# A fused attention and ternary feed-forward kernel: TensorE's units of a round in another order

## Chip, cores and metric

One core of a Trainium2 chip runs the whole kernel. The metric is device time of one execution in microseconds (us), the median of several runs. The profile is of one further execution with its own time.

## What is computed

The input x has 4 batches of 1024 rows of 128 numbers. The rows are normalised (xn) and go through causal attention with 16 heads of width 64 and through a linear layer with a ternary matrix and quantised input; both results are added to x.

```python
xn = _layernorm(x)
# attention
q, k, v = heads(xn @ Wq), heads(xn @ Wk), heads(xn @ Wv)
w = softmax(q @ k.T / DH + causal)
w = w * mask                       # a ramp over the keys, one span per head
w = w / (sum(w) + 1e-08)
att = (w @ v) @ Wo
# feed-forward
x_int = clip(round(xn / scale), -127, 127)
ffn = nan_to_num(x_int * scale) @ (ternary_weight - 1).T + bias
out = x + att + ffn
```

## The kernel before, in words

**Pairs and rounds.** Two heads of one batch make a pair: 4 batches of 8 pairs, 32 pairs in all. The plans at the top of the file (lines 36 to 54) give each engine's order for one round of the loop; a `+` or `-` behind a name means the next or the last pair. While the scores of pair i are worked on, the projections and maxima of pair i+1 are made and the division and output of pair i-1 are finished. `walk` (line 90) expands the plans; the FIRST plans run ahead of round 0, the LAST plans replace the plans in the last round. Nothing is scheduled at run time: each engine takes its units in the written order, and semaphores hold a unit back.

**The units on TensorE (PE).** Q and K are projections of a pair (lines 937 to 941, six matmuls each with 512 columns), V the values (lines 955 to 957, twelve of 256). M0 to M11 are products for the row maxima (line 968, one matmul for each of the two heads, side by side in the array). S0 to S11 are the score tiles (line 1006, four such pairs of matmuls; the exponent's shift is subtracted as the fourth). G3, G7 and G11 multiply four probability tiles each with the values (line 1023), D0 and D1 sum the denominators of each half of the queries (line 1038), Y0 and Y1 multiply the normalised values with Wo (line 1065; for the last pair of a batch the feed-forward's products at line 1053 go first). T turns the maxima (lines 975, 976), X0 and X1 turn the normalised rows of the next batch, four 128-column transposes each (line 922), W turns the ternary matrix once (line 1110).

**Shapes of the array.** Q, K, V, T, X, W and Y use the array as 128 x 128 (shown as 128\*128, T as 128\*16). M and S use it as two arrays of 64 rows (64\*128), one for each head. G and D use two arrays of 64 columns (128\*64). In program order TensorE changes between these three kinds fourteen times a round.

**The ring.** Q, K, V, M and S write to three slots of PSUM, two banks each, in turn (`IN_RING`, `NSLOT` = 3). A unit may start only when the unit three places before it in the ring has been read out: a score tile by ScalarE's exponential (E, line 567, with `exp_done`), a maximum by VectorE (R, lines 768 and 772, with `max_read`), V by VectorE's weighted copy (Vs, line 755, `v_done`), Q and K by VectorE's remainder (line 744). A further bank, `beside`, holds T, D, Y, X and W in turn, and `pv` holds the products of G. In `slot_left` (line 881) and `beside_left` (line 898) stand these waits.

```python
unit, j = IN_RING[n - NSLOT]
if unit[0] == "S":
    pe.wait_ge(exp_done, tiles_upto(j, int(unit[1:])))
elif unit[0] == "M":
    pe.wait_ge(max_read, j * NM + int(unit[1:]) + 1)
```

**The other engines.** ScalarE (ACT) makes the high parts of Q and K (line 556), the exponentials, and logarithm and inverse of the denominators (ln, ex, lines 573 and 578). VectorE (DVE) makes the remainders, the maxima R0 to R11 (R0 to R3 and R8 to R11 by two custom instructions with a mask, R4 to R7 by one reduction of 1024 numbers), the weighted values Vs, two steps of division (t, u, lines 792 and 797), the normalised values (o, line 804), the sum into the output (Ya, line 813) and one of seven steps of the quantisation for each pair (q, lines 700 to 712). GpSimd (POOL) zeroes the upper triangle of diagonal tiles (L, line 474), sums the probabilities over keys (A, lines 497 and 501) and adds the bias (B, line 463).

**Rows of the next batch.** In rounds 4 and 5 of a batch, X0 and X1 are turned into `beside`; ScalarE copies each half twice (high part, whole value `xf`), and VectorE makes the remainder.

Of the kernel before, what the change touches and what calls it, by code (L numbers as in the profile page):

```python
# [5 lines left out]
ALU = mybir.AluOpType  # L6
# [26 lines left out]

PE_PLAN = ("T Q+ K+ X0 X1 W G11- M0+ M1+ S0 S1 S2 M2+ D1- M3+ S3 V+ S4 S5 M4+ S6 M5+ Y1- M6+ M7+ S7 D0 G3 "
           "M8+ S8 S9 S10 M9+ Y0 M10+ M11+ S11 G7")
ACT_PLAN = "Z Qhi+ Khi+ X0 X1 E0 E1 E2 ln1- ex1- E3 E4 E5 E6 E7 ln0 ex0 E8 E9 E10 E11"
DVE_PLAN = ("Tc Z Qlo+ Klo+ R0+ R1+ X0 X1 W R2+ R3+ t1- u1- Vs+ o1- R4+ R5+ Ya1- R6+ R7+ t0 u0 R8+ o0 q "
            "R9+ R10+ Ya0 R11+")  # L40
POOL_PLAN = "L0 A0 L1 A1 L2 A2 L3 A3 A4 A5 A6 A7 L8 L9 L10 L11 A8 A9 A10 A11 B"

PE_FIRST = ("Q+ K+ I0+ I1+ M0+ M1+ M2+ I2+ M3+ I3+ M4+ I4+ M5+ I5+ H+ M6+ I6+ M7+ I7+ M8+ I8+ M9+ I9+ M10+ I10+ "
            "M11+ S0+ S1+ T+ S2+ S3+ Q++ K++ V+")
DVE_FIRST = ("Qlo+ Klo+ R0+ R1+ R2+ R3+ R4+ Hc+ R5+ R6+ R7+ R8+ R9+ R10+ R11+ Tc+ keys+ scale+ "
             "Qlo++ Klo++ Vs+")
ACT_FIRST = "xf0+ Qhi+ xf1+ Khi+ keys+ rest+ Hrow+ wv+ E0+ E1+ E2+ E3+ Qhi++ Khi++"


PE_LAST = "T G11- S0 S1 S2 D1- S3 S4 S5 S6 Y1- S7 D0 G3 S8 S9 S10 S11 Y0 D1 F1 G7 G11 Y1"  # L50
POOL_LAST = "L0 A0 L1 A1 L2 A2 L3 A3 L8 L9 L10 L11"
DVE_LAST = "Tc t1- u1- o1- A5 Ya1- A6 A7 t0 u0 o0 A8 A9 Ya0 t1 u1 o1 Ya1"
SP_PLAN = "mrow kext+ store-"
SP_FIRST = "kext+"

# [10 lines left out]
           8: "rstd2", 9: "norm2a", 10: "norm2b", 11: "norm3a", 12: "norm3b"}  # L66


def happens(name, i):

    if name in ("X0", "X1"):
        return i % PAIRS_OF_BATCH == 4 + int(name[1:]) and i < N_PAIRS - PAIRS_OF_BATCH
    if name == "W":
        return i == 1
    if name == "F1":
        return i == LAST
    if name[0] == "I":
        return i == 0
    if name == "q":
        return i % PAIRS_OF_BATCH < PAIRS_OF_BATCH - 1  # L80
    if name == "Z":
        return i in STEP_OF
    if name == "B":
        return i in (6, 11, 14)
    if name == "store":
        return i % PAIRS_OF_BATCH == PAIRS_OF_BATCH - 1
    return True
# [15 lines left out]


PE_ORDER = list(walk(PE_PLAN, PE_FIRST, PE_LAST))
IN_RING = [("X", -2)] + [u for u in PE_ORDER if u[0][0] in "QKSMV" or u == ("D1", LAST)]
IN_BESIDE = [u for u in PE_ORDER if u[0][0] in "THDYXWF" and u not in (("D1", LAST), ("Y1", LAST))]
PLACE = {u: n for n, u in enumerate(IN_RING)}
PLACE_BESIDE = {u: n for n, u in enumerate(IN_BESIDE)}
NSLOT = 3  # L110
# [20 lines left out]
def attention_ffn(nc, x_dram, wq_dram, wk_dram, wv_dram, wo_dram, span_dram, tern_dram, bias_dram,  # L131
# [11 lines left out]
    with ctx:  # L143
# [243 lines left out]
        def _(pool):  # L387
# [75 lines left out]
                g.tensor_tensor(rows, rows, bias_b[:, :].unsqueeze(1).to_broadcast([P, KB, P]), ALU.add  # L463
                                ).then_inc(bias_added, 1)

            pool.wait_ge(maxrow_done, 1)
            add_bias(0)

            def select(i, t):

# [33 lines left out]
            for name, i in walk(POOL_PLAN, "", POOL_LAST):  # L504
                if name[0] == "L":
                    select(i, int(name[1:]))
                elif name[0] == "A":
                    add(i, int(name[1:]))
                else:
                    add_bias((6, 11, 14).index(i) + 1)  # L510

        @block.scalar
        def _(act):
# [29 lines left out]
            def turned_whole(b, c, src):

                if b > 0:
                    act.wait_ge(fq_step, (b - 1) * FQ_STEPS + 1)
                else:
                    act.wait_ge(x2_done, c + 1)
# [47 lines left out]
            for name, i in walk(ACT_PLAN, ACT_FIRST):  # L596
                if name in ("Qhi", "Khi"):
                    high_parts(i, i % 2, name[0])
                elif name[0] == "E":
                    exps(i, int(name[1:]))  # L600
                elif name[:2] == "ln":
                    logarithms(i, int(name[2:]))
                elif name[:2] == "ex":
                    inverses(i, int(name[2:]))
                elif name[0] == "X":
                    turned_high(batch_of_turn(i), int(name[1:]), beside[:, :])
                    turned_whole(batch_of_turn(i), int(name[1:]), beside[:, :])
                elif name[:2] == "xf":
                    turned_whole(0, int(name[2:]), ring[:, slot("X", -2), int(name[2:]), :])
                elif name == "rest":  # L610
                    for n in range(2):
                        weights(w1[n][:, P:H * DH], w_raw[n][:, P:H * DH], w_rest_landed, 32, w_hi_done)
                elif name == "keys":
                    key_logarithms()
                elif name == "Hrow":
                    act.wait_ge(ext_done, 16 * NEXT)
                    act.wait_ge(first_rows_done, 1)
                    for h in range(2):
                        act.dma_start(mrow[0][h * DH:h * DH + 1, 0:HALF].bitcast(F32),
                                      first_rows[:, h * P:(h + 1) * P].bitcast(F32)).then_inc(first_rows_landed, 16)  # L620
                elif name == "wv":
                    weights(wv1[:, :], wv_raw, wv_landed, 16, wv_hi_done)
                elif STEP_OF[i] == "var1+":
                    rstd_start(2, slice(KB, 2 * KB))
                elif STEP_OF[i] == "rstd2":
                    rstd_start(3, slice(2 * KB, NB))

        @block.vector
        def _(dve):
# [40 lines left out]
            def turned(b, c, src):  # L670

                cols = slice(c * HALF, (c + 1) * HALF)
                dve.wait_ge(x1_done if b == 0 else xf_done, 2 * b + c + 1)
                v.tensor_tensor(x2[b % 2][:, cols], src, x1[b % 2][:, cols].bitcast(F32), ALU.subtract
                                ).then_inc(x2_done, 1)

# [165 lines left out]
            for name, i in walk(DVE_PLAN, DVE_FIRST, DVE_LAST):  # L842
                if name in ("Qlo", "Klo"):
                    low_parts(i, i % 2, name[0])
                elif name == "Vs":
                    weighted_values(i)
                elif name[0] == "R":
                    maxima(i, i % 2, int(name[1:]))
                elif name == "Tc":
                    maxima_out(i)  # L850
                elif name == "Hc":
                    first_rows_out()
                elif name == "scale":
                    quantisation_scale()
                elif name[0] == "A":
                    add_last(int(name[1:]))
                elif name[0] == "t":
                    newton_first(i, int(name[1:]))
                elif name[0] == "u":
                    newton_second(i, int(name[1:]))  # L860
                elif name[0] == "o":
                    normalise_values(i, int(name[1:]))
                elif name[:2] == "Ya":
                    add_output(i, int(name[2:]))
                elif name == "q":
                    quantise(i // NPB, i % NPB + 1)
                elif name[0] == "X":
                    turned(batch_of_turn(i), int(name[1:]), beside[:, :])
                elif name == "Z":
                    layer_norm_rest(STEP_OF[i])  # L870
                elif name == "keys":
                    key_weights()
                else:
                    dve.wait_ge(ternT_ready, 1)
                    v.tensor_copy(ternT[:, :], beside[:, 0:P]).then_inc(ternT_done, 1)

        @block.tensor
        def _(pe):
            t_ = nc.tensor

            def slot_left(name, i):
# [9 lines left out]
                elif unit in "QK":  # L891
                    pe.wait_ge(low_done, 2 * j + "QK".index(unit) + 1)
                elif unit == "V":
                    pe.wait_ge(v_done, j + 1)
                else:
                    pe.wait_ge(xf_done, 2)

            def beside_left(name, i):

# [9 lines left out]
                    pe.wait_ge(rden_done, halves_upto(j, int(unit[1:])))  # L909
                elif unit[0] == "Y":  # L910
                    pe.wait_ge(y_added, halves_upto(j, int(unit[1:])))
                elif unit[0] == "X":
                    pe.wait_ge(x2_done, 2 * batch_of_turn(j) + int(unit[1:]) + 1)
                else:
                    pe.wait_ge(ternT_done, 1)

# [161 lines left out]
            for name, i in PE_ORDER:  # L1078
# [57 lines left out]
```

## Time and profile before

| | |
|---|---|
| median of 3 runs | 1001.96 us (1001.88 to 1002.1) |
| profiled execution, its own time | 1001.64 us |
| its span in the profile | 999.9 us |
| TensorE busy | 985.0 us (99%) |
| VectorE busy | 757.3 us (76%) |
| GpSimd busy | 707.5 us (71%) |
| ScalarE busy | 451.7 us (45%) |
| mean granted TensorE clock | 0.997 |

Matmuls overlap in the records: one of 512 columns is shown as about 0.39 us long, and the next pair starts 0.23 us after it. So a busy TensorE says only that something is in the array; what a unit costs is read from start to start. Two matmuls of one unit that lie side by side in the array start within 0.01 us of each other. The timeline merges consecutive instructions of one form into one row with their count.

### The profile page before, as it was taken

Reading aid. Unit: us, or ns where it says so; the run is one execution under the profiler, and the core shown is the slowest. Engines: PE = TensorE matmul, PEld = TensorE weight load, DVE = VectorE, ACT = ScalarE, POOL = GpSimd, SP = SyncE. Lnnn points to the kernel's source line nnn. Section 1 sums busy time; section 2 is a strip of 40 time slices with the busy share of each in tenths; the row PEclk is TensorE's granted clock in tenths of the full one; section 3 lists DMA queues with packets and bytes.
Section 4 is the critical chain, followed back from the end, with each engine's and each line's share of the span. In section 5 each row is a group of like instructions: output and inputs, shape, how many; then the busy total and the mean of one; then the engine's idle time right before and its main releaser. Section 6 shows DMA issues by size and latency. Waiting matters only on the chain.

```text
span 999.9 us, 19209 instructions
## 1 busy us (share of the span) xinstructions
PE 985.0 (99%) x7121; PEld 634.2 (63%) x7121; DVE 757.3 (76%) x1706; ACT 451.7 (45%) x607; POOL 707.5 (71%) x649
## 2 busy tenths in 40 slices
PE   8899999999999999999999999999999999999997
PEld 4666666666666666666666666666666666666654
DVE  7877888878788878777767777777877667777754
ACT  4344445444454444454443454444454444454442
POOL 8766867667767668767767767667767667777672
PEclk9999999999999999999999999999999999999999
DMA  6000000000000000000000000000000000000000
GB/s 176 3 2 2 2 1 3 2 3 2 2 22 3 2 2 2 1 3 2 3 12 13 1 3 2 2 2 3 1 2 23 3 2 2 1 2 2 2 2 22
DMA packets 16133, 8.52 MB, mean 9 GB/s; under 512 B 5404, under 2 KB 15644, under 8 KB 16040
## 3 DMA queue, kind: packets, MB, share of 16 engines
q1 hardware_dynamic: 15416, 7.15, 2.7%
q8 instruction: 57, 0.93, 0.4%
q14 instruction: 36, 0.29, 0.1%
q10 hardware_dynamic: 624, 0.14, 0.1%
HBM read 4.33 MB, written 2.10 MB: 6 GB/s over the span
## 4 chain that ended last, share of the span: by engine, by line
PE 87%; DVE 8%; issue 2%; POOL 1%; ACT 1%; DMA 1%; DVEq 0%; SPq 0%; ACTq 0%; POOLq 0%
PE pv L1023 25%; PE ring L1006 24%; PE ring L968 12%; PE beside L1065 7%; PE beside L1038 6%; PE ring L941 3%; PE ring L937 3%; PE ring L938 3%; DVE ring L768 3%; DVE v L755 2%; DVE beside L792 1%; PE ring L955 1%; PE beside L1053 1%; PE ring L956 1%; PE ring L957 1%
## 5 line engine op out<-in xcount | busy, mean ns | idle before, releaser
L567 ACT ACTIVATE prob<-ring 128x1024 f32<-128x1024 f32 (+3 forms) x384 | 293.6, 810 | 347.9 <-PE ring L1006 347.7
L501 POOL TENSOR_TENSOR psumd<-psumd,prob 128x512 f32<-128x512 f32 (+1 forms) x250 | 406.4, 1626 | 28.9 <-POOL psumd L501 1.3
L768 DVE CUSTOM_DVE_ANT_0 ring<-ring,causal 128x128 f32<-128x128 f32 (+3 forms) x512 | 240.3, 517 | 96.7 <-PE ring L968 96.2
L1006 PE MATMUL ring<-q,k 64*128 64x512 f32 (+3 forms) x2304 | 279.5, 347 | 1.7 <-DMA mrow<-maxrow 0.8
L1023 PE MATMUL pv<-prob,v 128*64 128x512 f32 (+3 forms) x1536 | 267.1, 490 | 0.0
L474 POOL TENSOR_SCALAR_AFFINE_SELECT prob<-prob 128x256 f32<-128x256 f32 x256 | 110.1, 432 | 216.1 <-ACT prob L567 214.1
L1006 PEld LDWEIGHTS ring<-q,k 64*128 64x128 f32 x2304 | 194.6, 185 | 37.3 <-DVE rowmax L768 5.1
L1023 PEld LDWEIGHTS pv<-prob,v 128*64 128x64 f32 x1536 | 104.9, 137 | 154.1 <-issue 142.4
L772 DVE TENSOR_REDUCE rowmax<-ring 128x2 f32<-128x1024 f32 x128 | 151.5, 1222 | 4.8 <-PE ring L968 1.3
L497 POOL TENSOR_TENSOR psumd<-prob 128x768 f32<-128x768 f32 (+1 forms) x63 | 132.6, 2105 | 24.3 <-ACT prob L567 19.1
L968 PE MATMUL ring<-k,q 64*128 64x512 f32 (+3 forms) x768 | 143.9, 410 | 4.2 <-DVE k L744 1.5
L1006 PE MATMUL ring<-mrow,kext 64*128 64x512 f32 (+3 forms) x768 | 133.6, 342 | 0.0
L968 PEld LDWEIGHTS ring<-k,q 64*128 64x128 f32 x768 | 64.9, 184 | 74.2 <-ACT prob L567 27.7
L556 ACT ACTIVATE q<-ring 128x1024 fp32r<-128x1024 f32 x32 | 32.9, 1028 | 143.6 <-PE ring L941 143.6
L1006 PEld LDWEIGHTS ring<-mrow,kext 64*128 64x128 f32 x768 | 73.2, 185 | 7.7
L1065 PE MATMUL beside<-wo,o 128*128 128x128 f32 x512 | 73.4, 286 | 1.1 <-DVE o L804 1.1
L768 DVE DVE_READ_ACCUMULATOR2_ANT rowmax<- 128x1 f32 x512 | 72.5, 142 | 0.0
L1065 PEld LDWEIGHTS beside<-wo,o 128*128 128x128 f32 x512 | 62.0, 191 | 13.9 <-issue 9.2
L792 DVE TENSOR_TENSOR beside<-beside,r 128x512 f32<-128x512 f32 x63 | 45.0, 715 | 32.9 <-ACT r L578 32.8
L744 DVE TENSOR_TENSOR q<-ring,q 128x1024 fp32r<-128x1024 f32 x32 | 39.1, 1222 | 40.1 <-ACT q L556 40.0
L1038 PE MATMUL beside<-psumd,ones 128*64 128x512 f32 x252 | 68.0, 617 | 0.9 <-POOL psumd L501 0.9
L937 PE MATMUL ring<-x,w 128*128 128x512 f32 x128 | 53.0, 414 | 0.0
(120 smaller groups left out, 947.0 us busy)
## 6 DMA issues: line engine op xcount, KB each, us to landing
kext<-kext SPq DMA_DIRECT2D x128, 4.0 KB, 1.7
out<-x_sb SPq DMA_DIRECT2D x8, 256.0 KB, 2.4
x_sb<-in_L_attn_query SPq DMA_DIRECT2D x3, 512.0 KB, 5.5
mrow<-maxrow SPq DMA_DIRECT2D x62, 4.0 KB
x_sb<-in_L_attn_query SPq DMA_DIRECT2D x2, 256.0 KB, 4.0
xn_sb<-in_L_attn_Wv SPq DMA_DIRECT2D x1, 512.0 KB, 5.5
wo<-in_L_attn_Wo SPq DMA_DIRECT2D x1, 512.0 KB, 7.0
xn_sb<-in_L_attn_Wq SPq DMA_DIRECT2D x1, 448.0 KB, 3.5
```

The source lines that it names most:

```text
L474: g.affine_select(out=d, in_=d, compare_op=ALU.is_ge, fill=0.0, base=0, pattern=[[0, 2], [1, P]], channel_multiplier=-1).then_inc(sel_done, 1)
L497: g.tensor_tensor(acc[:, :, lo:HALF], before[:, :, lo:HALF], pr[:, :, lo:HALF], ALU.add).then_inc(acc_done, 2)
L501: g.tensor_tensor(acc[:, :, lo:HALF], acc[:, :, lo:HALF], pr[:, :, lo:HALF], ALU.add).then_inc(acc_done, 1)
L567: a.activation(prob[n % NPROB][:, :, lo:HALF], ring[:, slot(f"S{t}", i), :, lo:HALF], ACT.Exp, scale=1.0 / DH).then_inc(exp_done, 1)
L768: last = v.tensor_tensor_reduce(out=ring[:, s, h, 0:n], in0=ring[:, s, h, 0:n], in1=causal[:, HALF - n:HALF], scale=1.0, scalar=MASKED, op ...
L772: last = v.tensor_reduce(dst[:, :, 0], ring[:, s, :, 0:n], axis=AX, op=ALU.max)
L937: t_.matmul(ring[:, s, c, :], w1[n][:, cols], xa[:, rows], start=True, stop=False)
L968: last = t_.matmul(ring[:, s, h, 0:n], q1[p][rows, j * P:(j + 1) * P], k1[p][rows, k0:k0 + n], start=True, stop=True)
L1006: last = t_.matmul(ring[:, s, h, lo:HALF], k[p][rows, keys], q[p][rows, cols], start=(at == 0), stop=(at == len(parts) - 1))
L1023: last = t_.matmul(pv[h * DH:(h + 1) * DH, lo:HALF], v_sb[i // 2 % 2][:, kb, i % 2 * 2 + h, :], prob[(i * NT + t) % NPROB][:, h, lo:HALF], ...
L1038: last = t_.matmul(out[h * DH:(h + 1) * DH, :], ones[:, :], psumd[c][:, h, :], start=True, stop=not direct)
L1065: last = t_.matmul(beside[:, k * P:(k + 1) * P], o_sb[c][:, k * P:(k + 1) * P], wo[:, i % NPB, :], start=not with_ffn, stop=(not with_ffn ...
```

## The change

All of it is order, except for the turned rows. In a round, D1 of the last pair follows G11 at once; S3 and S4 follow S2; M2 and M3 come behind S4; Y1 and V follow M3 (with X, if there is one); S7 comes ahead of M6 and M7. The changes of the array's shape in a round are then: into G11 and D1, into M0, into Y1 and V, into S5, into D0, into M8, into Y0, into M10, into G7, into T, which is ten. VectorE's, ScalarE's and GpSimd's orders follow: q stands behind the remainder of K, R0 and R1 before t1, u1 and o1, R2 and R3 before Ya1 and Vs; ln and ex of the last pair stand before E0; A8 stands before L9.

X is now one unit of eight transposes in the ring, in round 4 of a batch. ScalarE makes only the high part from it; the whole value `xf` is made by GpSimd as the sum of both parts. In the first plans, S4 of pair 0 and M0 and M1 of pair 1 with two idle products between them are moved ahead of round 0, and the first bias comes behind A3 of pair 0.

```diff
-PE_PLAN = ("T Q+ K+ X0 X1 W G11- M0+ M1+ S0 S1 S2 M2+ D1- M3+ S3 V+ S4 S5 M4+ S6 M5+ Y1- M6+ M7+ S7 D0 G3 "
+PE_PLAN = ("T Q+ K+ G11- D1- M0+ M1+ S0 S1 S2 S3 S4 M2+ M3+ Y1- V+ X S5 M4+ S6 M5+ W S7 M6+ M7+ D0 G3 "
            "M8+ S8 S9 S10 M9+ Y0 M10+ M11+ S11 G7")
-ACT_PLAN = "Z Qhi+ Khi+ X0 X1 E0 E1 E2 ln1- ex1- E3 E4 E5 E6 E7 ln0 ex0 E8 E9 E10 E11"
-DVE_PLAN = ("Tc Z Qlo+ Klo+ R0+ R1+ X0 X1 W R2+ R3+ t1- u1- Vs+ o1- R4+ R5+ Ya1- R6+ R7+ t0 u0 R8+ o0 q "
-            "R9+ R10+ Ya0 R11+")
-POOL_PLAN = "L0 A0 L1 A1 L2 A2 L3 A3 A4 A5 A6 A7 L8 L9 L10 L11 A8 A9 A10 A11 B"
+ACT_PLAN = "Z Qhi+ Khi+ ln1- ex1- E0 E1 E2 E3 E4 X E5 E6 E7 ln0 ex0 E8 E9 E10 E11"
+DVE_PLAN = ("Tc Z Qlo+ Klo+ q R0+ R1+ t1- u1- o1- R2+ R3+ Ya1- Vs+ X R4+ W R5+ R6+ R7+ t0 u0 R8+ o0 R9+ "
+            "R10+ Ya0 R11+")
+POOL_PLAN = "L0 L1 L2 A0 L3 A1 A2 A3 B0 A4 A5 A6 A7 L8 A8 L9 L10 L11 A9 A10 A11 B xf"
@@
-            "M11+ S0+ S1+ T+ S2+ S3+ Q++ K++ V+")
+            "M11+ S0+ S1+ T+ S2+ S3+ Q++ K++ V+ S4+ M0++ I11+ M1++ I12+")
@@
-ACT_FIRST = "xf0+ Qhi+ xf1+ Khi+ keys+ rest+ Hrow+ wv+ E0+ E1+ E2+ E3+ Qhi++ Khi++"
-PE_LAST = "T G11- S0 S1 S2 D1- S3 S4 S5 S6 Y1- S7 D0 G3 S8 S9 S10 S11 Y0 D1 F1 G7 G11 Y1"
+ACT_FIRST = "xf0+ Qhi+ xf1+ Khi+ keys+ rest+ Hrow+ wv+ E0+ E1+ E2+ E3+ Qhi++ Khi++ E4+"
+PE_LAST = "T G11- D1- S0 S1 S2 S3 S4 Y1- S5 S6 S7 D0 G3 S8 S9 S10 S11 Y0 D1 F1 G7 G11 Y1"
@@
-DVE_LAST = "Tc t1- u1- o1- A5 Ya1- A6 A7 t0 u0 o0 A8 A9 Ya0 t1 u1 o1 Ya1"
+DVE_LAST = "Tc t1- u1- o1- q Ya1- A5 A6 A7 t0 u0 o0 A8 A9 Ya0 t1 u1 o1 Ya1"
@@
-IN_RING = [("X", -2)] + [u for u in PE_ORDER if u[0][0] in "QKSMV" or u == ("D1", LAST)]
-IN_BESIDE = [u for u in PE_ORDER if u[0][0] in "THDYXWF" and u not in (("D1", LAST), ("Y1", LAST))]
+IN_RING = [("X", -2)] + [u for u in PE_ORDER if u[0][0] in "QKSMVX" or u == ("D1", LAST)]
+IN_BESIDE = [u for u in PE_ORDER if u[0][0] in "THDYWF" and u not in (("D1", LAST), ("Y1", LAST))]
@@ gpsimd
-            pool.wait_ge(maxrow_done, 1)
-            add_bias(0)
+            def rows_of_parts(b):
+
+                pool.wait_ge(x2_done, 2 * b + 2)
+                pool.wait_ge(fq_step, (b - 1) * FQ_STEPS + 1)
+                g.tensor_tensor(xf[:, :], x1[b % 2][:, :].bitcast(F32), x2[b % 2][:, :].bitcast(F32), ALU.add
+                                ).then_inc(xf_done, 2)
@@ scalar
-                    turned_high(batch_of_turn(i), int(name[1:]), beside[:, :])
-                    turned_whole(batch_of_turn(i), int(name[1:]), beside[:, :])
+                elif name == "X":
+                    for c in range(2):
+                        turned_high(batch_of_turn(i), c, ring[:, slot("X", i), c, :])
@@ vector
-                dve.wait_ge(x1_done if b == 0 else xf_done, 2 * b + c + 1)
+                dve.wait_ge(x1_done, 2 * b + c + 1)
@@
-                    quantise(i // NPB, i % NPB + 1)
+                    quantise(i // NPB, i % NPB)
@@ tensor
+                else:
+                    pe.wait_ge(x2_done, 2 * batch_of_turn(j) + 2)
```

## Rows read from the trace of the kernel before

**Rows 1.** The page's first part: busy time, its share and instructions of each engine

```profile
PE 985.0 (99%) x7121; PEld 634.2 (63%) x7121; DVE 757.3 (76%) x1706; ACT 451.7 (45%) x607; POOL 707.5 (71%) x649
```

**Rows 2.** Timeline of PE, round of pair 18: start us, us, instruction, count

```profile
577.01 2.37 PE L1023 MATMUL pv<-prob,v 128*64 128x512 f32 x16
579.31 0.50 PE L968 MATMUL ring<-k,q 64*128 64x128 f32 x4
579.65 0.86 PE L1006 MATMUL ring<-q,k 64*128 64x512 f32 x6
...
581.85 0.44 PE L968 MATMUL ring<-k,q 64*128 64x384 f32 x2
582.23 1.08 PE L1038 MATMUL beside<-psumd,ones 128*64 128x512 f32 x4
583.24 0.50 PE L968 MATMUL ring<-k,q 64*128 64x512 f32 x2
583.57 0.45 PE L1006 MATMUL ring<-q,k 64*128 64x128 f32 x6
...
584.06 0.38 PE L955 MATMUL ring<-wv,x 128*128 128x256 f32 x1
...
585.68 0.98 PE L1006 MATMUL ring<-q,k 64*128 64x512 f32 x6
...
586.72 0.87 PE L1006 MATMUL ring<-q,k 64*128 64x512 f32 x6
...
587.84 0.51 PE L968 MATMUL ring<-k,q 64*128 64x512 f32 x2
588.19 0.85 PE L1006 MATMUL ring<-q,k 64*128 64x512 f32 x6
...
589.11 0.40 PE L968 MATMUL ring<-k,q 64*128 64x512 f32 x2
589.43 1.16 PE L1065 MATMUL beside<-wo,o 128*128 128x128 f32 x8
590.52 0.73 PE L968 MATMUL ring<-k,q 64*128 64x512 f32 x4
591.10 0.86 PE L1006 MATMUL ring<-q,k 64*128 64x512 f32 x6
...
592.11 0.65 PE L1038 MATMUL beside<-psumd,ones 128*64 128x512 f32 x2
```

**Rows 3.** Timeline of DVE in the same round

```profile
582.49 0.57 DVE L768 CUSTOM_DVE_ANT_0 ring<-ring,causal 128x384 f32<-128x384 f32 x1 [1.28 <-PE ring L968]
...
583.49 0.14 DVE L768 DVE_READ_ACCUMULATOR2_ANT rowmax<- 128x1 f32 x1
583.93 0.70 DVE L768 CUSTOM_DVE_ANT_0 ring<-ring,causal 128x512 f32<-128x512 f32 x1 [0.30 <-PE ring L968]
...
585.20 0.73 DVE L792 TENSOR_TENSOR beside<-beside,r 128x512 f32<-128x512 f32 x1
...
586.57 1.22 DVE L755 TENSOR_TENSOR v<-ring,vtab 128x1024 f32<-128x1024 f32 x1
...
588.50 2.39 DVE L772 TENSOR_REDUCE rowmax<-ring 128x2 f32<-128x1024 f32 x2
590.80 0.68 DVE L813 TENSOR_TENSOR x_sb<-x_sb,beside 128x512 f32<-128x512 f32 x1
```

**Rows 4.** Timeline of ACT: the first two exponentials of the same round, merged

```profile
580.77 1.73 ACT L567 ACTIVATE prob<-ring 128x1024 f32<-128x1024 f32 x2 [2.63 <-PE ring L1006]
```

**Rows 5.** Timeline of PE: the four transposes of an X unit, and G11

```profile
426.01 0.60 PE L922 MATMUL beside<-ident,xn_sb 128*128 128x128 f32 x4
426.54 2.37 PE L1023 MATMUL pv<-prob,v 128*64 128x512 f32 x16
```

**Rows 6.** Windows of round 0: length, busy us of each engine, clock, DMA share, GB/s

```profile
36.00:40.00 4.00, 2.41 (x13) 1.23 (x11) 4.00 (x12) 0.13 (x1) 3.83 (x5) 0.84 0.01 3
40.00:42.60 2.60, 2.60 (x14) 2.41 (x12) 2.34 (x9) 0.00 (x0) 0.62 (x1) 0.58 0.00 0
```

More of the change, by code:

```diff
@@ L66 @@
            8: "rstd2", 9: "norm2a", 10: "norm2b", 11: "norm3a", 12: "norm3b"}
+BIAS_AT = (0, 6, 11, 14)
 def happens(name, i):
-    if name in ("X0", "X1"):
-        return i % PAIRS_OF_BATCH == 4 + int(name[1:]) and i < N_PAIRS - PAIRS_OF_BATCH
+    if name in ("X", "xf"):
+        return i % PAIRS_OF_BATCH == (4 if name == "X" else 5) and i < N_PAIRS - PAIRS_OF_BATCH
     if name == "W":
@@ L79, in happens @@
     if name == "q":
-        return i % PAIRS_OF_BATCH < PAIRS_OF_BATCH - 1
+        return i % PAIRS_OF_BATCH > 0
     if name == "Z":
@@ L83, in happens @@
     if name == "B":
-        return i in (6, 11, 14)
+        return i in BIAS_AT[1:]
+    if name == "B0":
+        return i == BIAS_AT[0]
     if name == "store":
@@ L508, in _ @@
                     add(i, int(name[1:]))
+                elif name == "xf":
+                    rows_of_parts(batch_of_turn(i - 1))
                 else:
-                    add_bias((6, 11, 14).index(i) + 1)
+                    add_bias(BIAS_AT.index(i))
         @block.scalar
@@ L541, in turned_high, with turned_whole @@
                 a.activation(x1[b % 2][:, c * HALF:(c + 1) * HALF], src, ACT.Copy).then_inc(x1_done, 1)
[L543 to L548, printed above, removed]
+            def turned_whole(c, src):
+                act.wait_ge(x2_done, c + 1)
                 a.activation(xf[:, c * HALF:(c + 1) * HALF], src, ACT.Copy).then_inc(xf_done, 1)
@@ L604, in _ @@
                     inverses(i, int(name[2:]))
-                elif name[0] == "X":
-                    turned_high(batch_of_turn(i), int(name[1:]), beside[:, :])
-                    turned_whole(batch_of_turn(i), int(name[1:]), beside[:, :])
+                elif name == "X":
+                    for c in range(2):
+                        turned_high(batch_of_turn(i), c, ring[:, slot("X", i), c, :])
                 elif name[:2] == "xf":
-                    turned_whole(0, int(name[2:]), ring[:, slot("X", -2), int(name[2:]), :])
+                    turned_whole(int(name[2:]), ring[:, slot("X", -2), int(name[2:]), :])
                 elif name == "rest":
@@ L865, in _ @@
                 elif name == "q":
-                    quantise(i // NPB, i % NPB + 1)
-                elif name[0] == "X":
-                    turned(batch_of_turn(i), int(name[1:]), beside[:, :])
+                    quantise(i // NPB, i % NPB)
+                elif name == "X":
+                    for c in range(2):
+                        turned(batch_of_turn(i), c, ring[:, slot("X", i), c, :])
                 elif name == "Z":
@@ L894, in slot_left @@
                     pe.wait_ge(v_done, j + 1)
+                elif j < 0:
+                    pe.wait_ge(xf_done, 2)
                 else:
-                    pe.wait_ge(xf_done, 2)
+                    pe.wait_ge(x2_done, 2 * batch_of_turn(j) + 2)
             def beside_left(name, i):
@@ L911, in beside_left @@
                     pe.wait_ge(y_added, halves_upto(j, int(unit[1:])))
-                elif unit[0] == "X":
-                    pe.wait_ge(x2_done, 2 * batch_of_turn(j) + int(unit[1:]) + 1)
                 else:
@@ L1105, in _ @@
                     output_projection(i, int(name[1:]))
-                elif name[0] == "X":
-                    turn(batch_of_turn(i), int(name[1:]), beside[:, :])
+                elif name == "X":
+                    for c in range(2):
+                        turn(batch_of_turn(i), c, ring[:, slot("X", i), c, :])
                 else:
```

## The prediction, made before the changed kernel was run

> **What bounds the kernel now.** I read the page first: TensorE is busy 99% of the span, no other engine over 76% [rows 1]. That alone says little, because matmuls overlap in the records. So I took PE's timeline of one quiet round (pair 18, no turned rows, no feed-forward) and read every unit from start to start [rows 2]. It holds almost nothing but matmul work, and two kinds of small loss that the waits view hardly shows.
>
> The first loss is a change of the array's shape. M5's pair of 512 columns (589.11) is followed by Y1 after 0.32 us; four such pairs of S6 with its successor take 588.19 to 589.11, or 0.23 each. So the boundary costs 0.09. Behind it, the first step of the new shape is slow too: S4, first behind V, takes 1.04 (585.68 to 586.72), S6, in the middle of its stretch, 0.92. I call this 0.12 the refill. After D1, M3 takes 0.33 to S3 instead of 0.23. One change thus costs 0.2; into D and G the refill is smaller (I take 0.05), and out of them the boundary is 0.10.
>
> The second loss is a late slot. M4 starts at 587.84; VectorE's weighted values ended at 586.57 + 1.22 = 587.79 [rows 3]. S5 to M4 takes 1.12 instead of 0.92, so 0.20 is wait, and M4 to S6 takes 0.35 instead of 0.23: **a wait pays the refill again**. A unit starts 0.05 after the recorded end of its releaser.
>
> **What the new order gives.** It drops one entry into D1 (0.09 + 0.05), one exit from it (0.10 + 0.12) and one way into and out of 128 x 128 (2 x 0.21): 0.78 a round. M4's wait on V with its refill (0.32) also goes, since M4 now follows M3 in its slot. Together 1.10.
>
> The Trainium skill ("TensorEngine Tiling (Array Packing)", Key Properties) says that changing the tiling mode drains the engine; "TensorE: Matmul & The Clock Gate", Step-by-step, gives the array's drain as some 128 cycles. Estimated from these two pages a change would be 0.05 us at 2.4 GHz and four fewer would save 0.2 a round, 6 us in all, not 0.78 a round; the trace has durations for the boundary and for the refill, so they are used.
>
> **What it costs: three late slots.** A ring of three slots asks that a unit, and the two behind it, last as long as its read-out. I lay the new order out from G11 to D0, each term from one round [rows 2 to 4]:
>
> - G11 to D1: 2.30 less the boundary 0.10 = 2.20. D1 to M0: D1 to M3 is 1.01, less the refill 0.05 = 0.96. M0 to S0: 0.34.
> - S0 to S4: S4 takes the slot of S1 and needs E1. E1 ended at 580.77 + 1.73 = 582.50, 2.85 behind S0 [rows 2, 4], so S4 starts at 2.90. TensorE alone would be there at 2.64: S0 to S2 2.20 (579.65 to 581.85), S3 four pairs of 0.11. A wait of 0.26 appears. E0's release of S3 is as tight as it was for M2, which stood there.
> - S4 to M2: 1.04, refill included.
> - M2 to S6: S6 takes V's slot. VectorE starts R2 0.54 behind M2 (0.64 less the refill that M2 had), R2 takes 1.00 (582.49 to 583.49), R3 1.27 (583.93 to 585.20), Ya1 0.59 (0.68 less the 0.09 by which R5's end at 590.89 overlaps it), Vs 1.22; with 0.05 that is 4.67 [rows 3]. TensorE would need 4.29: M2 0.18, M3 0.32, Y1 1.00 (1.09 less its exit), V 1.52 (1.62 less its refill), S5 1.04, M4 0.23. Wait: 0.38.
> - S6 to M5: 0.92 + 0.12 = 1.04.
> - M5 to M7: M7 takes M5's slot and needs R5. M4 to R4 is 588.50 - 587.84 = 0.66, less 0.12 = 0.54; the reduction takes 1.24; with 0.05, 1.83. S7 and M6 between them fill only 0.23 + 0.92 + 0.23 = 1.38. Wait: 0.45. Before, Y1 lay here and gave the time.
> - M7 to D0: 0.32 and 0.11 of refill = 0.43.
>
> The sum is 15.41; the trace has 592.11 - 577.01 = 15.10. **A round gets 0.31 longer**: 1.10 gained, 0.26 + 0.38 + 0.45 waited and three refills (0.36) paid; without these 1.45 it would be 13.98, 1.12 shorter (the last 0.02 is rounding). Thirty rounds hold all of these units: +9.3.
>
> The same skill page (TensorEngine Tiling, Performance Considerations) warns that PSUM copies may become the bottleneck once TensorE is made faster by tiling. That speaks against this change in kind: every new wait above is a read-out. By the page alone there is no size.
>
> **The rest.** Everything behind D0 keeps its order on TensorE and nothing there is tight: 0. GpSimd's reordered tail only brings A11, and with it D1, forward: 0; were that cover gone, D1 would hold TensorE by what A11 lacks. The step q now lies between the remainder of K and R0; its longest form fits into the 0.86 (2.20 + 0.96 - 2.30) by which M0 comes later: 0, up to 0.1 in two rounds of eight. The first plan: S4's 1.04 goes into the stretch where TensorE is busy 2.41 of 4.00 us, and V, which ran behind it at a granted clock of 0.58, most of it at the lower level of 1.2 GHz, can run at the full 2.4 GHz; 2.60 x 0.42 = 1.09 is the most that this gives back [rows 6]. I take -2.1, bounds -2.3 and -0.5. The idle products lie in waits. Turned rows: two rounds of a batch each spent 0.53 - 0.09 = 0.44 on X [rows 5]; one round now spends 0.88, and the slot stays taken until ScalarE's and VectorE's two halves are through, which no row shows in this place. Bounds: -0.3 (X bridges V's wait) and +1.5 (two high parts and two remainders in series, less S5, M4); I take +0.3, three times: +0.9. GpSimd's sum for `xf` and the bias behind A3 move work on an engine with idle time: 0. Last round: two fewer changes, against score tiles that now follow each other and wait for exponentials; 0, bounds -0.6 and +1.
>
> Sum: 9.3 - 2.1 + 0.9 = +8.1 on the profiled 1001.64, that is 1009.7. The median of the runs lies 0.32 above the profiled time, so I forecast **1010 us**.
>
> **Rivals.**
> *Faster, the read-outs keep up.* Waits and refills of 1.45 decide against a gain of 1.12; with the -1.2 of the rest spread over the rounds the turning point is 1.16. If a slot were free well before the recorded end of its read-out, none of the waits would stand: 30 x -1.12 - 1.2 gives 967; with half of them left, 989. For it: engines other than TensorE idle a quarter of the time [rows 1]. Against it: M4 started 0.05 behind Vs to the hundredth, and M5 to M7 is a chain of three rows with no slack to find.
> *No change, the refill is not paid after these waits.* If the weights of S4, S6 and M7 are in before the release, 0.36 a round goes: 1010 - 10.8 = 999. M4 speaks against it.
> *Slower than forecast, turned rows.* At +1.5 a batch and with the start giving only 0.5, the sum is 1015.
> *The change does not do what it says.* Counting the plans gives ten changes; I give this nothing.
>
> **How the numbers follow.** Forecast case 0.58; refill not paid 0.13 (between 997 and 1003); more than forecast 0.09; read-outs keep up 0.20. Within 0.2% (2 us, about what a measurement of this kernel can tell from no change) is 1000 to 1004: 0.13. Slower: 0.66. Faster: 0.21. The forecast's own range is 1004 to 1014, from 0.1 a round in the terms and the bounds of the rest. To leave out no more than 2 in 10 it is stretched to 997 and 1015.
>
> **What would show it.** Right: D1 straight behind G11, and D0 15.4 behind G11; S4 0.05 behind the end of E1, S6 behind Vs, M7 behind R5, each followed by a slow first step; waits of score units on exponentials and of maxima on reductions; V of round 0 at the full clock. Wrong: S6 and M7 starting without a gap (first rival), or the gaps there with a first step of 0.23 (second).

## The result and the profile after

The changed kernel takes 1012.6 us (median of 4 runs, 1011.45 to 1018.1) where the kernel before takes 1001.92: a ratio of 1.0115, 95% interval 1.0091 to 1.0139. It is slower. The profiled execution has 1012.66 us and a span of 1010.9, 11.0 more than before.

The page first: busy times, then the chain that ended last by engine. TensorE is as busy as before [rows 1].

```profile
PE 987.0 (98%) x7125; PEld 627.2 (62%) x7125; DVE 751.9 (74%) x1706; ACT 452.2 (45%) x601; POOL 708.2 (70%) x652
...
PE 81%; DVE 11%; issue 4%; POOL 2%; ACT 1%; DMA 0%; SPq 0%; DVEq 0%; POOLq 0%; ACTq 0%
```

The last line, which read 87% for PE and 8% for DVE before, says where it goes: the chain runs more often through another engine. PE's timeline of the round of pair 18 shows the places, in the columns of [rows 2]:

```profile
579.23 2.37 PE L1032 MATMUL pv<-prob,v 128*64 128x512 f32 x16
581.43 1.03 PE L1047 MATMUL beside<-psumd,ones 128*64 128x512 f32 x4
582.39 0.50 PE L977 MATMUL ring<-k,q 64*128 64x128 f32 x4
...
585.63 0.96 PE L1015 MATMUL ring<-q,k 64*128 64x512 f32 x6
586.67 0.56 PE L977 MATMUL ring<-k,q 64*128 64x384 f32 x4
...
590.71 0.40 PE L977 MATMUL ring<-k,q 64*128 64x512 f32 x2
591.36 0.96 PE L1015 MATMUL ring<-q,k 64*128 64x512 f32 x6 [0.25 <-DVE v L763]
...
593.67 1.04 PE L977 MATMUL ring<-k,q 64*128 64x512 f32 x4
594.63 0.65 PE L1047 MATMUL beside<-psumd,ones 128*64 128x512 f32 x2
```

From the top: G11, D1, M0 and M1, ..., S4, M2 and M3, ..., M4, S6, ..., M6 and M7, D0. G11 to D0 takes 594.63 - 579.23 = 15.40 us; before it was 15.10. D1 stands directly behind G11. S4 waits for E1, ScalarE's second exponential:

```profile
584.78 0.80 ACT L575 ACTIVATE prob<-ring 128x768 f32<-128x768 f32 x1
```

It ends at 585.58, and S4 starts at 585.63. M4 (590.71) to S6 (591.36) is 0.65 instead of 0.23: S6 waits for the weighted values. M6 and M7 together last 1.04 in the merged row; M6 and M7 in [rows 2] lasted 0.73. VectorE's timeline shows who is late:

```profile
590.09 1.22 DVE L763 TENSOR_TENSOR v<-ring,vtab 128x1024 f32<-128x1024 f32 x1
591.26 1.23 DVE L780 TENSOR_REDUCE rowmax<-ring 128x2 f32<-128x1024 f32 x1
592.93 1.23 DVE L780 TENSOR_REDUCE rowmax<-ring 128x2 f32<-128x1024 f32 x1 [0.44 <-PE ring L977]
```

Vs ends at 591.31, S6 starts at 591.36. R5 ends at 594.16, and M7 can start only behind that; its row is merged, but 593.67 + 1.04 - 0.50 puts it at 594.21. VectorE itself idled 0.44 ahead of R5: TensorE and VectorE wait for each other in turn through three slots.

By stretches (start of T to start of T): the round of pair 0 went from 29.83 to 27.94 us (-1.89), the thirty rounds behind it from 902.96 to 911.22 (+8.26), the last round with the store from 36.40 to 41.04 (+4.64). Sum: 11.0.

The last round is a surprise. GpSimd's timeline of L1 and, further down, A3 in the kernel before:

```profile
970.69 0.41 POOL L474 TENSOR_SCALAR_AFFINE_SELECT prob<-prob 128x256 f32<-128x256 f32 x1
...
976.25 0.72 POOL L501 TENSOR_TENSOR psumd<-psumd,prob 128x256 f32<-128x256 f32 x1
```

And in the changed kernel:

```profile
977.06 1.29 POOL L483 TENSOR_SCALAR_AFFINE_SELECT prob<-prob 128x256 f32<-128x256 f32 x1
...
983.49 1.57 POOL L510 TENSOR_TENSOR psumd<-psumd,prob 128x256 f32<-128x256 f32 x1
```

The same select L1 takes 1.29 instead of 0.41, and the last sum A3 1.57 instead of 0.72. What VectorE does beside them, q's first step and then the sums A6 and A7:

```profile
976.77 1.36 DVE L720 COPY_PREDICATED fq<-xn_sb,big 128x1024 f32<-128x1024 uint32 x1
...
983.25 2.90 DVE L847 TENSOR_TENSOR psumd<-psumd,prob 128x1024 f32<-128x1024 f32 x2
```

D0 waits for A3. PE's timeline there, D0 and G3, before:

```profile
977.12 1.08 PE L1038 MATMUL beside<-psumd,ones 128*64 128x512 f32 x4 [0.85 <-POOL psumd L501]
978.00 2.35 PE L1023 MATMUL pv<-prob,v 128*64 128x512 f32 x16
```

The same after:

```profile
985.21 1.97 PE L1047 MATMUL beside<-psumd,ones 128*64 128x512 f32 x4 [3.62 <-POOL psumd L510]
986.95 4.40 PE L1032 MATMUL pv<-prob,v 128*64 128x512 f32 x16
```

And the windows of the wait and of D0 and G3 after (columns as in [rows 6]):

```profile
981.20:985.20 4.00, 0.40 (x4) 0.02 (x1) 3.79 (x3) 1.47 (x2) 3.79 (x3) 0.89 0.00 0
985.20:991.20 6.00, 5.99 (x20) 2.41 (x20) 2.34 (x3) 1.23 (x2) 0.00 (x0) 0.51 0.00 0
```

TensorE idled 3.62 us, and then ran D0 and G3 at a granted clock of 0.51, which is the lower of its two levels, 1.2 GHz. D0 comes 1.73 us later behind the last T (15.40 against 13.67), and from D0's start to the next score tile's it is 6.07 us (985.21 to 991.28) instead of 3.16.

VectorE's last plan was changed in two places: q stands in it for the first time (the kernel before makes this step one round earlier), and Ya1 stands ahead of the sum A5 instead of between A5 and A6.

### The profile page after: what moved, and what is told of

It is laid out like the page before. It is cut to its first block, busy times and chain, and to the rows that moved or that the text cites. A ratio compares the mean times of both kernels' runs of the same rounds, so it can differ in the third digit from the quotient of the medians.

```text
span 1010.9 us, 19214 instructions
## 1 busy us (share of the span) xinstructions
PE 987.0 (98%) x7125; PEld 627.2 (62%) x7125; DVE 751.9 (74%) x1706; ACT 452.2 (45%) x601; POOL 708.2 (70%) x652
## 4 chain that ended last, share of the span: by engine, by line
PE 81%; DVE 11%; issue 4%; POOL 2%; ACT 1%; DMA 0%; SPq 0%; DVEq 0%; POOLq 0%; ACTq 0%
PE pv L1032 25%; PE ring L1015 25%; PE ring L977 9%; PE beside L1047 6%; PE beside L1074 4%; PE ring L946 3%; DVE v L763 3%; PE ring L950 3%; PE ring L947 3%; DVE ring L776 2%; DVE rowmax L780 1%; DVE x_sb L821 1%; POOL psumd L506 1%; DVE rowmax L776 1%; PE beside L1062 1%
## 5 line engine op out<-in xcount | busy, mean ns | idle before, releaser
L1015 PE MATMUL ring<-q,k 64*128 64x512 f32 (+3 forms) x2304 | 289.4, 356 | 9.8 <-DVE v L763 6.7
L483 POOL TENSOR_SCALAR_AFFINE_SELECT prob<-prob 128x256 f32<-128x256 f32 x256 | 104.8, 422 | 237.8 <-ACT prob L575 235.3
L1015 PEld LDWEIGHTS ring<-q,k 64*128 64x128 f32 x2304 | 184.6, 185 | 63.8 <-DVE v L763 18.7
L780 DVE TENSOR_REDUCE rowmax<-ring 128x2 f32<-128x1024 f32 x128 | 153.8, 1223 | 19.0 <-PE ring L977 18.9
L977 PE MATMUL ring<-k,q 64*128 64x512 f32 (+3 forms) x768 | 136.7, 391 | 2.7 <-DVE k L752 0.7
L977 PEld LDWEIGHTS ring<-k,q 64*128 64x128 f32 x768 | 67.2, 184 | 71.7 <-issue 32.6
L581 ACT ACTIVATE lnden<-beside 128x512 f32<-128x512 f32 x63 | 37.7, 598 | 104.9 <-PE beside L1047 104.9
```

Source lines behind the costliest of these rows:

```text
L483: g.affine_select(out=d, in_=d, compare_op=ALU.is_ge, fill=0.0, base=0, pattern=[[0, 2], [1, P]], channel_multiplier=-1).then_inc(sel_done, 1)
L780: last = v.tensor_reduce(dst[:, :, 0], ring[:, s, :, 0:n], axis=AX, op=ALU.max)
L977: last = t_.matmul(ring[:, s, h, 0:n], q1[p][rows, j * P:(j + 1) * P], k1[p][rows, k0:k0 + n], start=True, stop=True)
L1015: last = t_.matmul(ring[:, s, h, lo:HALF], k[p][rows, keys], q[p][rows, cols], start=(at == 0), stop=(at == len(parts) - 1))
```

## The experiments

**One part alone: D1 behind G11 in the kernel before.** Twelve changes of shape.

```diff
-PE_PLAN = ("... W G11- M0+ M1+ S0 S1 S2 M2+ D1- M3+ S3 V+ ...
+PE_PLAN = ("... W G11- D1- M0+ M1+ S0 S1 S2 M2+ M3+ S3 V+ ...
-ACT_PLAN = "Z Qhi+ Khi+ X0 X1 E0 E1 E2 ln1- ex1- E3 ...
+ACT_PLAN = "Z Qhi+ Khi+ X0 X1 ln1- ex1- E0 E1 E2 E3 ...
-DVE_PLAN = ("... R0+ R1+ X0 X1 W R2+ ...
+DVE_PLAN = ("... X0 X1 W R0+ R1+ R2+ ...
```

> The kernel before with one part of the change alone: D1 of the last pair follows G11 at once (ln and ex stand before E0, and VectorE's X0, X1 and W before R0, so that nothing blocks). TensorE changes shape twelve times a round instead of fourteen. Theory of the ring's read-outs: 0.36 us of shape changes are saved, but D1 was what lay between the score tiles and M3; M3 now stands in S1's slot at S0 + 2.38 and waits for E1 until S0 + 2.90, 0.52 of wait and 0.12 of refill, and S3 behind it waits for E2 by some 0.15. So a round gets 0.4 to 0.5 longer and the kernel takes 1013 to 1017 us. Rival, that the number of shape changes is what counts: 30 x 0.36 less, 991 us.

Measured: 1020.4 us, 1.0176 (1.0138 to 1.0214). A quiet round takes 30.20 instead of 29.74, +0.46 as reckoned. PE's timeline at M2 and M3:

```profile
591.72 0.44 PE L968 MATMUL ring<-k,q 64*128 64x384 f32 x2
592.41 0.49 PE L968 MATMUL ring<-k,q 64*128 64x512 f32 x2 [0.26 <-ACT prob L567]
```

M2 to M3 is 0.69 (0.18 unhindered): the wait for E1. The kernel came out 3 us above the range given; its last round is 39.76 (+3.4), which I had not reckoned. The plan of TensorE's last round still has D1 behind S2, while ScalarE now makes ln and ex, which need D1, before E0. So S3 waits for E0, and D0 comes 3.37 later behind the last T than before (17.04 against 13.67). PE's timeline, S3 in the last round:

```profile
988.35 0.56 PE L1006 MATMUL ring<-q,k 64*128 64x128 f32 x6 [2.27 <-ACT prob L567]
```

Fewer changes of shape and a slower kernel: the rival is out.

**One part undone: S7 behind M6 and M7.** Ten changes, as in the changed kernel.

```diff
-... M5+ W S7 M6+ M7+ D0 G3
+... M5+ W M6+ M7+ S7 D0 G3
```

> The changed kernel with one part undone: M6 and M7 ahead of S7 as before, the rest as changed; ten changes of shape. Theory of the read-outs: M7 takes S6's slot and waits for E6 until S6 + 2.31 (TensorE would be there at 1.50), S7 takes M5's and waits for R5 until S6 + 2.87 (there at 2.65), D0 comes 1.13 behind it at S6 + 4.00 instead of S6 + 3.30. So 0.70 a round longer, 1012.6 + 21 = 1033 us. Rival, that the place of S7 within one shape does not matter: 1012.6 us.

Measured: 1033.3 us, 1.0308 (1.0265 to 1.0351). PE's timeline, M5 and M6 in the first row, M7 in the second; below them D0 and G3 of the last round:

```profile
604.84 0.65 PE L977 MATMUL ring<-k,q 64*128 64x512 f32 x4
606.12 0.49 PE L977 MATMUL ring<-k,q 64*128 64x512 f32 x2 [0.63 <-ACT prob L575]
...
1006.56 1.97 PE L1047 MATMUL beside<-psumd,ones 128*64 128x512 f32 x4 [3.64 <-POOL psumd L510]
1008.30 2.98 PE L1032 MATMUL pv<-prob,v 128*64 128x512 f32 x16
```

M7 waits for E6, as the theory has it, and the time is met to 0.3 us, with some luck: in the profile the thirty rounds are 20.7 longer and round 0 is 0.65 longer, but the last round, whose plans are the same, is 1.4 shorter. The same work in the same shapes, one unit moved by two places: +21 us.

**VectorE's order alone.**

```diff
-DVE_PLAN = ("... R2+ R3+ Ya1- Vs+ X R4+ W R5+ R6+ ...
+DVE_PLAN = ("... R2+ R3+ Vs+ X R4+ R5+ Ya1- W R6+ ...
```

> The changed kernel with VectorE's order alone altered: Vs directly behind R3, Ya1 behind R5. S6's wait for V falls from 0.38 to about 0.10. Theory: VectorE has no free time between R2 and R5, so the wait only moves: R4 comes later against S6 and S7 waits for it by about 0.2, D0 waits for Ya1 by about 0.15; the round stays within 0.1 and the kernel within 3 us of 1012.6. Rival, that S6's wait stands alone on the path: 0.28 a round less, 1004 us.

Measured: 1010.2 us. S6 now follows M4 after 0.36 (590.63 to 590.99) instead of 0.65, but M5 to S7 grew from 0.23 to 0.45. PE's timeline, M5 and S7:

```profile
592.02 0.41 PE L977 MATMUL ring<-k,q 64*128 64x512 f32 x2
592.47 0.96 PE L1015 MATMUL ring<-q,k 64*128 64x512 f32 x6
```

The thirty rounds take 909.83 us instead of 911.22: 1.4 us are won of the 8 that the wait looked worth. The wait moved. The rest of the 2.4 lies in the last round (39.79 instead of 41.04), whose plans are unchanged.

**The new first plans alone, in the kernel before.**

```diff
-PE_FIRST = ("... Q++ K++ V+")
+PE_FIRST = ("... Q++ K++ V+ S4+ M0++ I11+ M1++ I12+")
-ACT_FIRST = "... Qhi++ Khi++"
+ACT_FIRST = "... Qhi++ Khi++ E4+"
```

> The kernel before with the new first plans of TensorE and ScalarE alone (S4 of pair 0, M0 and M1 of pair 1 and two idle products ahead of round 0). Theory: nothing but round 0 changes; S4 fills a gap (about 0.4 to 1.0 us) and V runs at the full clock (up to 1.1 us): the stretch from the first T to the second takes 28 to 28.5 us instead of 29.8, the kernel 1.3 to 1.8 us less, 1000.5 us. Rival, that round 0 is shorter only because of the new order of the round: no change, 1002.

Measured: 1000.7 us against 1001.87, ratio 0.999 (0.9981 to 1.0). The first T to the second takes 28.84, 1.0 less, short of what I expected. Windows of the two stretches of [rows 6]:

```profile
36.00:40.00 4.00, 3.78 (x24) 2.17 (x22) 3.88 (x10) 1.10 (x2) 3.83 (x5) 1.00 0.01 3
40.00:42.60 2.60, 2.60 (x22) 2.08 (x20) 2.47 (x9) 0.00 (x0) 0.60 (x1) 1.00 0.00 0
```

V ran at the full clock (0.58 before), yet part of the time won is waited away later in the round: waits of 0.56 and 0.66 us stand where the kernel before has one of 0.36. The interval reaches 1.0, and 5 of the 21 runs of the kernel before beside it took 1000.68 to 1000.79 us, as long as these (1000.50 to 1000.79). So the run times don't show that the new plans save more than V's lower clock costs; no trace shows what the clock was in those five. The other 0.9 of the changed kernel's 1.89 came with the round's new order; which part of it, no run shows.

**The last round, three tries**, all in the changed kernel's last plan of VectorE; the added lines are, from the top, q early, q late, and sums clear:

```diff
-DVE_LAST = "Tc t1- u1- o1- q Ya1- A5 A6 A7 t0 ...
+DVE_LAST = "Tc q t1- u1- o1- Ya1- A5 A6 A7 t0 ...
+DVE_LAST = "Tc t1- u1- o1- Ya1- A5 A6 A7 q t0 ...
+DVE_LAST = "Tc t1- u1- o1- A5 Ya1- A6 A7 q t0 ...
```

> The changed kernel with VectorE's quantisation step q in the last round moved from behind o1 to the front, behind Tc; nothing else. In the changed kernel the last round took 4.6 us more than before from T to the end. Theory: q, a predicated copy of 1.35 us, held GpSimd's L1 (1.29 instead of 0.41), the sums A1 to A3 and with them D0 came later, TensorE idled 3.6 us before D0 and its granted clock fell to the lower level for D0 and G3. With q moved, the last round is back at 36.4 us and the kernel at 1008 us. Rival, that the new order of ln and ex before E0, or of D1, delays the last round's sums: no change, 1012.6.

Measured: median 1013.4 us (1010.92 to 1017.68), too wide a spread for a verdict; the profile decides. The last round took 39.52: L1 was back at 0.41, but q ran beside A11, which took 1.61 instead of 0.72, D1 started 3.08 behind T instead of 2.52, and D0 still 15.10.

> The changed kernel with the last round's quantisation step q behind A7 (VectorE waits there for the inverse) instead of behind o1; nothing else. The try with q at the front gave back only part, because there the predicated copy ran against GpSimd's A11 and held D1 by 0.56, and the sums stayed late. Theory: with q away from every GpSimd instruction L1 takes 0.41 again (1.29 in the changed kernel), A3 ends before VectorE's second sum begins and takes 0.72 (1.57), D0 starts 13.7 behind the last T (15.4), and TensorE keeps the full clock over D0 and G3; the last round is back near 36.4 us, the kernel 4 us below the changed one, 1008 to 1009 us. Rival, that the orders of D1, ln and ex delay the sums: the last round stays at 39 us or more and the kernel at 1011 or more.

Measured: 1010.4 us, 1.0087 (1.0074 to 1.0099); last round 38.93. Half right: L1 took 0.41 and D0 came at 14.51, but A3 stayed at 1.57, since without q VectorE's second sum A6 began just ahead of it. GpSimd's L3 and A3:

```profile
980.99 1.40 POOL L483 TENSOR_SCALAR_AFFINE_SELECT prob<-prob 128x256 f32<-128x256 f32 x1
982.47 1.57 POOL L510 TENSOR_TENSOR psumd<-psumd,prob 128x256 f32<-128x256 f32 x1
```

> As the try with q behind A7, and in the last round Ya1 stands between VectorE's sums A5 and A6 again, as in the kernel before. With q moved alone D0 still started 14.51 behind the last T, since GpSimd's A3 took 1.57 while VectorE's A6 ran beside it; in the kernel before Ya1 held A6 back and A3 took 0.72. Theory: A3 takes 0.72 to 0.8, D0 starts at 13.7, TensorE's granted clock stays at the full level over D0 and G3, the last round takes 36.3 to 36.8 us (38.9 with q moved alone, 41.0 in the changed kernel) and the kernel 1008 us. Rival, that the clock falls from the order of score tiles and not from the longer wait ahead of D0: the last round stays near 38.9.

Measured: 1007.9 us, 1.0066 (1.0053 to 1.0079); last round 36.37, D0 at 13.64. GpSimd's A3:

```profile
982.61 0.72 POOL L510 TENSOR_TENSOR psumd<-psumd,prob 128x256 f32<-128x256 f32 x1
```

And the windows over the wait and over D0 and G3:

```profile
982.10:984.40 2.30, 0.93 (x6) 0.44 (x8) 2.30 (x3) 0.58 (x1) 1.15 (x2) 1.00 0.00 0
984.40:986.70 2.30, 2.30 (x20) 1.23 (x16) 2.20 (x3) 1.23 (x2) 0.00 (x0) 1.00 0.00 0
```

The order of D1, ln and ex is as in the changed kernel here, so that rival is out: the 4.6 us of the last round are VectorE's place beside GpSimd, and the clock. Of the 1.73 by which D0 was late, q caused 0.89 (15.40 to 14.51) and Ya1's place 0.87 (14.51 to 13.64). The clock's part is less certain. With S7 behind M7 and with Vs first, the last round has the changed kernel's plans, TensorE idles 3.64 and 3.61 us and D0 comes at 15.40 too, but D0 to the next score tile takes 4.64 and 4.82 us, not 6.07, and the last round 39.61 and 39.79. So the last round costs 3.2 to 4.6 us more than before, as the clock falls, and q late alone (38.93) won 0.7 to 2.1.

**An order made by the theory.** Twelve changes of shape.

```diff
-... V+ X S5 M4+ S6 M5+ W S7 M6+ M7+ D0 G3 M8+ S8 S9 ... M10+ M11+ S11 G7
+... V+ X S5 S6 W M4+ D0 M5+ M6+ M7+ G3 M8+ S7 S8 S9 ... M10+ S11 M11+ G7
-DVE_PLAN = ("Tc Z Qlo+ Klo+ q R0+ R1+ ... R2+ R3+ Ya1- Vs+ X R4+ W R5+ R6+ R7+ t0 u0 R8+ o0 R9+ R10+ Ya0 R11+")
+DVE_PLAN = ("q Tc Z Qlo+ Klo+ R0+ R1+ ... R2+ R3+ Vs+ X Ya1- W R4+ R5+ R6+ R7+ R8+ t0 u0 o0 R9+ Ya0 R10+ R11+")
-ACT_PLAN = "... E5 E6 E7 ln0 ex0 E8 ...
+ACT_PLAN = "... E5 E6 ln0 ex0 E7 E8 ...
-POOL_PLAN = "L0 L1 L2 A0 L3 A1 A2 A3 B0 A4 A5 A6 A7 L8 A8 L9 L10 L11 A9 A10 A11 B xf"
+POOL_PLAN = "L0 L1 A0 L2 L3 A1 A2 A3 B0 A4 A5 A6 L8 L9 A7 L10 A8 L11 A9 A10 A11 B xf"
```

with q late in the last round.

> A new order made from the changed kernel by the theory of the read-outs: D0 lies between M4 and M5 and G3 between M7 and M8, S6 stands directly behind S5, S7 behind M8, Vs ahead of Ya1, the other engines to match, q of the last round behind A7. Twelve changes of the array's shape, two more than in the changed kernel. The slots of V, S5, S6, M4 and M5 are then reused only after other work has gone by (M2 to Vs 4.08 against 4.98 on TensorE, M4 to M7 1.90 against 1.83). Theory: the waits of S6 and M7 and their refills go (1.07 a round), two changes come (0.36 to 0.4), S4's wait on E1 stays: a round takes 29.35 us instead of 30.07, thirty of them 21 us less, with the last round's 4 us 987 to 989 us. Rival, that the number of changes decides: slower than the changed kernel by 30 x 0.4, 1020 us.

Measured: 1001.3 us, 0.9984 (0.9965 to 1.0004), not the 987 to 989 expected. Eleven rounds are right, 29.37 to 29.48 us; but seven take 29.91 to 30.00 (the next run's expectation counts ten), the thirty together 899.7 instead of the changed kernel's 911.2, 11.5 less where 21 were expected, and the last round takes 42.5. VectorE's q at the front of a round:

```profile
598.51 2.31 DVE L712 TENSOR_SCALAR fq<-fq,sc 128x1024 f32<-128x1024 f32 x1
```

GpSimd's sum and select at the same time:

```profile
597.89 2.38 POOL L510 TENSOR_TENSOR psumd<-psumd,prob 128x1024 f32<-128x1024 f32 x1
600.20 0.88 POOL L483 TENSOR_SCALAR_AFFINE_SELECT prob<-prob 128x256 f32<-128x256 f32 x1
```

The same q takes 0.74 in the kernel before; here it ends 0.55 behind the sum. The mended version has q behind Klo, and the kernel before's last round:

```diff
+PE_LAST = "T G11- S0 S1 S2 D1- S3 S4 S5 S6 Y1- S7 D0 ...
+ACT_LAST = "E0 E1 E2 ln1- ex1- E3 E4 E5 E6 E7 ln0 ex0 E8 ...
+DVE_LAST = "Tc t1- u1- o1- A5 Ya1- A6 A7 q t0 ...
```

> The covered order (1001.3 us) with two things mended. Its regular rounds took 29.37 as reckoned, but ten rounds took about 29.95: q, put at the front of the round, ran 2.3 us beside GpSimd's sums and made both late; and the last round took 42.5 us, because D1 waited there for A11 and the granted clock fell. Now q stands behind the remainder of K, where GpSimd is idle, and the last round has the kernel before's order on TensorE, ScalarE and VectorE (q behind A7). Theory: some 0.55 us come off in about ten to thirteen rounds (6 to 7 us) and 5.5 to 6 us off the last round: 988 to 990 us. Rival, that these rounds are late for their place in the batch and not for q: 995 us.

Measured: **992.1 us**, 0.9931 (0.9905 to 0.9957): faster than both kernels, 2 us above what I expected. The last round is 36.41; the second to fourth rounds fell from 29.91, 30.66 and 29.93 to 29.87, 30.21 and 29.41. Six of the seven rounds of 29.9 to 30.0 came back to 29.4, which speaks for q and against the rival. But the thirty rounds gained only 3.9 us, not 6 to 7: the rounds of pairs 6, 14 and 22 rose from 29.4 to 29.8 or 29.9, and those of pairs 7 and 15 from 30.9 to 31.4. GpSimd is not idle behind Klo there. In pair 22's round q's compare (0.68 in the changed kernel) takes 2.10 beside GpSimd's sum for `xf`, and R0 starts 0.64 later than in pair 18's (VectorE's row, then GpSimd's):

```profile
692.19 2.10 DVE L719 TENSOR_SCALAR xn_sb<-fq 128x1024 uint32<-128x1024 f32 x1
...
691.37 2.38 POOL L476 TENSOR_TENSOR xf<-x 128x1024 f32<-128x1024 f32 x1
```

In the rounds of pairs 7 and 15 it is a predicated copy (2.77 and 2.75) beside GpSimd's bias. Of the 9.7 us by which the profiled span is shorter than the kernel before's, 2.6 lie in round 0 and 7.2 in the thirty rounds. PE's timeline of pair 18: S6, ..., M4, D0, M5 to M7, G3:

```profile
582.65 0.85 PE L1016 MATMUL ring<-q,k 64*128 64x512 f32 x6
...
583.56 0.39 PE L978 MATMUL ring<-k,q 64*128 64x512 f32 x2
583.88 1.08 PE L1048 MATMUL beside<-psumd,ones 128*64 128x512 f32 x4
584.89 1.00 PE L978 MATMUL ring<-k,q 64*128 64x512 f32 x6
585.82 2.37 PE L1033 MATMUL pv<-prob,v 128*64 128x512 f32 x16
```

S6, M4 and the three maxima start without a wait; M5 to G3 takes 0.93, of which shape change, refill and three pairs explain 0.88.

## Why the prediction was right, and where it was off

*Shape changes and refill.* Right. G11 to D1 takes 2.20 (forecast 2.20), D1 to M0 0.96 (0.96), S4 to M2 1.04 (1.04).

*The three late slots.* Right. S0 to S4 takes 2.91 (2.90), M2 to S6 4.69 (4.67), S6 to M5 1.02 (1.04), M5 to D0 2.25 (1.83 + 0.43). The rival by which the read-outs keep up falls with S6, which starts 0.05 behind the end of Vs, and the one by which the refill is not paid falls with the 1.04 from S4 to M2; the undone S7 and the lone D1 confirm both by new waits of the size reckoned.

*"Thirty rounds hold all of these units: +9.3", and turned rows +0.9.* Slightly over: 8.26 instead of 10.2. Fifteen quiet rounds gained 0.34 each and the six with turned rows 3.16 in all (forecast 2.8). The three with a feed-forward fell by 0.14 in all: its products now lie between M3 and V and cover S6's wait. Six early rounds, in which VectorE normalises rows of later batches, grew by only 0.17 in all; they had been late before, and I had not looked at their rows one by one.

*"Its longest form fits into the 0.86".* It doesn't: q's longest form, a predicated copy, takes 1.35 us. It cost nothing all the same, since VectorE had idled another 0.44 us ahead of R0 in the kernel before: the rounds of pairs 7, 15 and 23, which are among those that have it, grew by 0.34 to 0.39, as the quiet ones.

*The start.* -2.1 was forecast and -1.89 measured, with V's clock as said. The size is partly luck: the sum named only the first plans, and these alone gave 1.0; I had not reckoned with the waits that come back behind them, nor with what the round's new order gives to round 0.

*"Last round: ... 0, bounds -0.6 and +1".* **This step failed**: +4.64. I weighed TensorE's changes against ScalarE's waits and did not look at GpSimd beside VectorE. The shift of q put a 1.36 us copy beside GpSimd's L1 (0.88), and Ya1's place ahead of A5 let VectorE's A6 start just ahead of A3 (0.85). That the second comes from Ya1 and not from q is shown by q late, where A3 still took 1.57. D0 came 1.73 later and the clock fell for another 2.9, in two other traces of the same last round for 1.5 and 1.7 only. The errors of the rounds and of the last round have opposite signs, so the total (11.0 in the profile, 8.1 forecast) looks better than that part deserves.

The Trainium skill ("GPSIMD Engine Reference", Specifications) says that GpSimd shares its SBUF interfaces with VectorE, with contention where a VectorE instruction runs in a two-port mode or has two SBUF inputs. The trace agrees: L1 takes 1.29 beside the predicated copy, which reads two tiles (xn_sb and big), and 0.41 without it.

## What to carry to other kernels

In a ring of n slots a unit's read-out must fit into the time of the n - 1 units behind it; before shape changes or other fixed costs are taken out, write down what each removed or moved unit was covering. Work of another kind (here D0, G3, Y1) is worth a change of shape where it fills such a time: twelve changes with cover beat ten without (a quiet round of 29.4 us against 30.07). When an order is altered, look at the first and last rounds with the same care, since they lack the cover that the regular ones have.

## What the runs showed of the hardware

A wait on TensorE costs more than its length: the first step behind it takes about 0.1 us more, as behind a change of shape (S4 and S6, each behind a wait in the changed kernel, take 1.04 and 1.02 where S6 before took 0.92). VectorE and GpSimd stretch each other in both directions: a select of 0.41 us took 1.29 to 1.40, a sum of 0.72 took 1.57, VectorE's step of 0.74 took 2.31 and its compare of 0.68 took 2.10 beside a GpSimd sum.

The clock: in the last round of the changed kernel TensorE idled 3.62 us and ran D0 and G3 at a granted 0.51. In two other runs it idled 3.64 and 3.61 us at the same place and ran them at 0.67 and 0.65, with D0 at 1.97 and 1.98 us instead of 1.08, but G3 at 2.98 and 3.16 (4.40 in the changed kernel, 2.35 before). With q early and q late it had idled 2.72 and 2.73 us; D0 took its usual 1.08, and the clock fell during G3 (0.65 over that stretch). With the sums clear it had idled 1.87 us and kept the full clock. From D0's start to the next score tile's that is 6.07, 4.64, 4.82, 4.86, 4.85 and 3.16 us. The idle time right before does not settle it alone: in the covered order an idle of 1.98 us ahead of the last round's D1 was followed by 3.2 us at a granted 0.58.
